# Graph-attention edge walks: the chain from logits to exponents spread over two chunks, four slots of gathered rows

## What is computed

```python
h = einsum('nd,dhf->nhf', x, W)
logits = leaky_relu(sum(h*a_src)[src] + sum(h*a_dst)[dst], 0.2)
m = segment_max(logits, dst)
e = exp(logits - m[dst])
z = segment_sum(e, dst)
out = segment_sum(h[src] * (e / (z[dst] + eps)), dst)
```

## Time and profile before

| | |
|---|---|
| median of 3 runs | 7074.7 us (7064.91 to 7080.67) |
| the profiled execution | 7060.18 us, span 7058.4 |
| PE busy | 4868.9 us (69%) |
| PE weight loads | 3367.9 (48%) |
| DVE | 3968.4 (56%) |
| ACT | 2368.3 (34%) |
| POOL | 2984.7 (42%) |
| mean granted TensorE clock | 0.815 of 2.4 GHz |
| gathers of line 783 | 832 in `l_edges`, 416 each in `l2a_edges` and `l2b_edges` |

### The profile page before, as it was taken

One profiled execution on the slowest core, in us unless ns is written; L12 is line 12 of the kernel. 1 busy time (PEld: TensorE's weight loads), 2 busy tenths in 40 slices (PEclk: granted clock), 3 DMA queues, 4 the chain that ended last, 5 costly groups with the idle time before them and its releaser, 6 DMA issues. The chain is left out here.

```text
span 7058.4 us, 80551 instructions
## 1 busy us (share of the span) xinstructions
PE 4868.9 (69%) x19231; PEld 3367.9 (48%) x19232; DVE 3968.4 (56%) x8601; ACT 2368.3 (34%) x5719; POOL 2984.7 (42%) x2932
## 2 busy tenths in 40 slices
PE   2676749547775947775577747888898555377999
PEld 2444426325543734444344434444577333265666
DVE  3555633446667246665466656667324788686333
ACT  1333312123333224433243424455221222174333
POOL 2555432445552045552655526666000777352000
PEclk8778859768787968888688868889999666697999
DMA  4454414234442034443444411111001999673000
GB/s 116 137 163 153 114 54 126 90 102 141 141 144 62 1 108 144 136 143 87 141 136 144 130 42 27 30 30 27 22 7 52 362 368 377 213 228 98 9 13 23
DMA packets 543458, 819.10 MB, mean 116 GB/s; under 512 B 87966, under 2 KB 421967, under 8 KB 542839
## 3 DMA queue, kind: packets, MB, share of 16 engines
q1 hardware_dynamic: 396388, 432.93, 19.0%
q0 software_dynamic: 140832, 376.78, 18.9%
q10 hardware_dynamic: 5907, 5.92, 0.3%
HBM read 658.06 MB, written 157.71 MB: 116 GB/s over the span
## 5 line engine op out<-in xcount | busy, mean ns | idle before, releaser
L783 POOL DMA_INDIRECT l_edges_stage<-l_h_rows,src_t x832 | 802.1, 964 | 682.7 <-issue 217.9
L1096 PE MATMUL l_edges_ps_sum<-l_edges_msg,l_edges_hot 128*128 128x264 f32 x1664 | 595.1, 500 | 275.7 <-DVE l_attn_acc L925 179.8
L2492 POOL DMA_INDIRECT l_edge_kv<-l_kv_rows,src_t x416 | 476.3, 1145 | 673.2 <-POOLq L2400 516.8
L2918 POOL DMA_INDIRECT l_gate_edges_srow<-l_gate_src_rows,l_gate_edges_idx x512 | 487.2, 952 | 329.7 <-issue 142.3
L3054 PE MATMUL l_gate_edges_ps<-l_gate_edges_wide,l_gate_edges_hot_lo 128*128 128x500 f32 x1024 | 505.6, 636 | 102.5 <-issue 72.0
L1096 PEld LDWEIGHTS l_edges_ps_sum<-l_edges_msg,l_edges_hot 128*128 128x128 f32 x1664 | 354.1, 238 | 438.0 <-DVE l_attn_acc L925 257.7
L2545 PE MATMUL l_edge_ps_q<-l_q_q,l_edge_hot 128*128 x832 | 341.2, 581 | 303.9 <-issue 211.4
L783 POOL DMA_INDIRECT l2a_edges_stage<-l2a_h_rows,src_t x416 | 400.0, 961 | 340.8 <-issue 118.1
L783 POOL DMA_INDIRECT l2b_edges_stage<-l2b_h_rows,src_t x416 | 400.7, 963 | 329.0 <-issue 116.1
L2545 PEld LDWEIGHTS l_edge_ps_q<-l_q_q,l_edge_hot 128*128 128x128 f32 x832 | 231.8, 292 | 413.2 <-issue 367.4
L1096 PE MATMUL l2a_edges_ps_sum<-l2a_edges_msg,l2a_edges_hot 128*128 128x272 f32 x832 | 303.4, 508 | 159.6 <-DVE l2a_sums_acc L925 106.9
(11 more groups left out here) (786 smaller groups left out, 10893.5 us busy)
## 6 DMA issues: line engine op xcount, KB each, us to landing
l_edge_e<-e_rows SPq DMA_DIRECT2D x416, 128.0 KB
l_val_rows<-l_edge_vj SPq DMA_DIRECT2D x104, 512.0 KB
l_agg_stage<-l_val_rows SPq DMA_DIRECT2D x52, 1024.0 KB, 5.6
l_edges_rel_b<-rel_rows SPq DMA_DIRECT2D x52, 512.0 KB
l_edges_ea<-in_edge_attr SPq DMA_DIRECT2D x48, 512.0 KB
e_rows<-l_edges_e_s SPq DMA_DIRECT2D x48, 512.0 KB
l_experts_w<-in_L_ffn_w SPq DMA_DIRECT2D x32, 512.0 KB, 5.0
l_gate_edges_lo_b<-l_gate_edges_lo_rows SPq DMA_DIRECT2D x64, 256.0 KB
```

The costliest lines, as they stand in the source:

```text
L783: nc.gpsimd.indirect_dma_start(out=stage[:, c % SL, u, :], out_offset=None, in_=h_rows, in_offset=bass.IndirectOffsetOnAxis(ap=K.src_t[:, ...
L1096: nc.tensor.matmul(ps_sum[u][:], hot[:, g, u, :], msg[:, g % 2, u, :], start=True, stop=True).then_inc(summed, 1)
L2492: nc.gpsimd.indirect_dma_start(out=kv[:, m, u, :], out_offset=None, in_=kv_rows, in_offset=bass.IndirectOffsetOnAxis(ap=K.src_t[:, n * EB ...
L2918: nc.gpsimd.indirect_dma_start(out=srow[:, n % 4, u, :], out_offset=None, in_=src_rows, in_offset=bass.IndirectOffsetOnAxis(ap=idx[:, n * ...
```

## The change

- The chain is stretched. In chunk c DVE runs `tile_tops(c+1)` right behind `rescale`, then `logits(c+2)`, weigh 1, `nodes_hot(c+3)`, the adds of group 0, weigh 2, `tile_ends(c+2)` mixed with the adds of group 1, `edge_maxima(c+1)`, weigh 3, the adds of group 2, `exponents(c+1)`, the adds of group 3. PE's products follow that order, and `expand(c+3)` stands behind the second `scatter`.
- `lgT` has two halves in `ps_w`, so that two chunks can be under way. The one semaphore that counted DVE's steps becomes four.
- `stage` has four slots (SL = 4). POOL's extra waits stay, now: group 1 of chunk c for the turned logits of c-2, group 2 for the placed tops of c-3, group 3 for the placed ends of c-2.
- `rel_b` has one slot, `e_s` half the rows (each half of a chunk's terms is stored by itself), and the zeros are a quarter as wide and sent with a repeated source.
- DVE's loop has four chunks (PER = 4) and five turns; the last six chunks are written out. PE's loop has one turn fewer.
- The first two chunks' chains run ahead of the loop.

The core of the diff (waits and scans of the same form are cut):

```diff
-    SL, PER = 3, 6
-    assert (NCK - 2) % PER == 0 and PER % SL == 0 and PER % 2 == 0
+    SL, PER = 4, 4
+    REST = 2
+    assert (NCK - REST) % PER == 0 and PER % SL == 0 and PER % 2 == 0
     with Phase(nc, name) as ph:
         stage = ph.sb("stage", [P, SL, CK, RW])
-        rel_b = ph.sb("rel_b", [P, 2, CK * P], BF16)
+        rel_b = ph.sb("rel_b", [P, CK * P], BF16)
...
-        e_s = ph.sb("e_s", [P, 2, EdgeTerms.PER_CHUNK, D])
+        e_s = ph.sb("e_s", [P, 2, EdgeTerms.PER_CHUNK // 2, D])
...
@@ -774,11 +778,11 @@
                         if c >= SL:
                             pool.wait_ge(msg_built, NG4 * (c - SL) + g + 1)
                             if g == 1:
-                                pool.wait_ge(lg_turned, c - SL + 2)
+                                pool.wait_ge(lg_turned, c - SL + 3)
                             elif g == 2:
-                                pool.wait_ge(ends_placed, c - SL + 2)
+                                pool.wait_ge(inits_made, c - SL + 2)
                             elif g == 3:
-                                pool.wait_ge(inits_made, c - SL + 2)
+                                pool.wait_ge(ends_placed, c - SL + 3)
...
-                def store(c):
-                    sp.wait_ge(e_kept, 2 * c + 3)
+                def store(c, h):
...
+                def rel(c):
+                    if c >= 1:
+                        sp.wait_ge(hotT_built, c)
+                    sp.dma_start(rel_b[:], over_partitions(K.rel_rows[c * CK:(c + 1) * CK, :].rearrange("s e -> (s e)"))).then_inc(rel_in, 16)
...
                 for c in range(NCK):
-                    if c >= 2:
-                        sp.wait_ge(hotT_built, c - 1)
...
+                    if c + 2 < NCK:
+                        rel(c + 2)
...
+                        store(-1, 1)
+                    if c >= 2:
+                        store(c - 2, 0)
+                        store(c - 2, 1)
...
                 def tile_ends(c, i, add):
                     cut_f, cut_r = (K.cuts[:, bass.ds(c, 1), a, :].rearrange("p c e -> p (c e)") for a in range(2))
                     dve.wait_ge(lg_turned, c + 1)
-                    nc.vector.tensor_tensor_scan(local[:, 1, :], cut_f, lgT, NEG, ALU.add, ALU.max).then_inc(dv, 1)
+                    if not (isinstance(c, int) and c == 0):
+                        dve.wait_ge(inits_made, c)
+                    nc.vector.tensor_tensor_scan(local[:, 1, :], cut_f, lgT[i % 2], NEG, ALU.add, ALU.max).then_inc(end_steps, 1)
...
-                def tile_tops(c, i, add):
+                def tile_tops(c, i):
...
+                def exponents(c, i, with_ends):
                     m = i % 2
+                    dve.wait_ge(f_placed, c + 1)
+                    if with_ends:
+                        dve.wait_ge(ends_placed, c + 2)
                     dve.wait_ge(max_turned, c + 1)
...
                     blks = block_ids(nc, mybir.EngineType.DVE, K, c)
                     rescale(c, blks[0])
                     if after >= 1:
-                        logits(c + 1, j, i + 1)
-                    for g, step in enumerate((tile_ends, tile_tops, edge_maxima)):
-                        weigh(c, i, g + 1)
-                        if after >= 1:
-                            step(c + 1, i + 1, adds(c, g, blks))
-                        else:
-                            for u in range(GR):
-                                adds(c, g, blks)(u)
+                        tile_tops(c + 1, i + 1)
+                    if after >= 2:
+                        logits(c + 2, j, i + 2)
+                    weigh(c, i, 1)
+                    if after >= 3:
+                        nodes_hot(c + 3, j, i + 3)
+                    for u in range(GR):
+                        adds(c, 0, blks)(u)
+                    weigh(c, i, 2)
+                    if after >= 2:
+                        tile_ends(c + 2, i + 2, adds(c, 1, blks))
+                    else:
+                        for u in range(GR):
+                            adds(c, 1, blks)(u)
                     if after >= 1:
-                        exponents(c + 1, i + 1)
-                    if after >= 2:
-                        nodes_hot(c + 2, j, i + 2)
+                        edge_maxima(c + 1, i + 1)
+                    weigh(c, i, 3)
                     for u in range(GR):
-                        adds(c, GR - 1, blks)(u)
+                        adds(c, 2, blks)(u)
+                    if after >= 1:
+                        exponents(c + 1, i + 1, after >= 2)
+                    for u in range(GR):
+                        adds(c, 3, blks)(u)
...
                 nodes_hot(0, 0, 0)
                 logits(0, 0, 0)
-                for step in (tile_ends, tile_tops, edge_maxima):
-                    step(0, 0, lambda u: None)
                 nodes_hot(1, 0, 1)
-                exponents(0, 0)
-                with dve.Fori(0, (NCK - 2) // PER) as j:
+                tile_ends(0, 0, lambda u: None)
+                tile_tops(0, 0)
+                logits(1, 0, 1)
+                nodes_hot(2, 0, 2)
+                tile_ends(1, 1, lambda u: None)
+                edge_maxima(0, 0)
+                exponents(0, 0, True)
+                with dve.Fori(0, (NCK - REST) // PER - 1) as j:
                     for i in range(PER):
-                        chunk(j * PER + i, j, i, 2)
-                chunk(NCK - 2, (NCK - 2) // PER, 0, 1)
-                chunk(NCK - 1, (NCK - 2) // PER, 1, 0)
+                        chunk(j * PER + i, j, i, 3)
+                LAST = (NCK - REST) // PER - 1
+                for i in range(PER + REST):
+                    c = LAST * PER + i
+                    chunk(c, LAST, i, min(3, NCK - 1 - c))
 
...
                 def chunk(c, m, after, j=None):
                     last_maxima(c, m, 0)
+                    if after:
+                        rescaling(c + 1, 1 - m)
                     for g in range(1, NG4):
                         if j is not None and g == 3:
                             keep_turned(c, 0)
                         edges_hot(c, g)
                         last_maxima(c, m, g)
                     if j is not None:
-                        keep_terms(c, m, 0, j * 16 + 16)
+                        keep_terms(c, m, 0, j * 32 + (16 * m + 16))
                     if after:
-                        rescaling(c + 1, 1 - m)
                         edges_hot(c + 1, 0)
                         if j is not None:
                             keep_turned(c, 1)
                         weights(c + 1)
                     if j is not None:
-                        keep_terms(c, m, 1, None)
+                        keep_terms(c, m, 1, j * 32 + (16 * m + 16))
...
                 def chunk(c, m, after, j=None):
                     scatter(c, 0)
+                    if after >= 2:
+                        turn_logits(c + 2, m)
                     if after >= 1:
-                        turn_logits(c + 1, 1 - m)
+                        place_tops(c + 1)
                     if after >= 2:
                         turn_attr(c, m, 0, j * 16 + 16 * (m + 1))
                     scatter(c, 1)
-                    if after >= 1:
-                        place_ends(c + 1)
+                    if after >= 3:
+                        expand(c + 3, m, block_ids(nc, mybir.EngineType.PE, K, c + 3))
                     if after >= 2:
                         attr_terms(c, 0)
                     scatter(c, 2)
-                    if after >= 1:
-                        place_tops(c + 1)
                     if after >= 2:
                         turn_attr(c, m, 1, None)
-                    scatter(c, 3, 0, GR // 2)
                     if after >= 1:
+                        turn_maxima(c + 1)
                         place_f(c + 1)
-                        turn_maxima(c + 1)
-                    scatter(c, 3, GR // 2)
                     if after >= 2:
-                        blks = block_ids(nc, mybir.EngineType.PE, K, c + 2)
+                        place_ends(c + 2)
+                    scatter(c, 3)
                     if after >= 2:
                         attr_terms(c, 1)
-                        expand(c + 2, m, blks)
...
                 last.then_inc(e_made, 1)
                 expand(0, 0, block_ids(nc, mybir.EngineType.PE, K, 0))
                 turn_logits(0, 0)
+                expand(1, 1, block_ids(nc, mybir.EngineType.PE, K, 1))
                 place_ends(0)
+                turn_logits(1, 1)
                 place_tops(0)
+                expand(2, 0, block_ids(nc, mybir.EngineType.PE, K, 2))
+                turn_maxima(0)
                 place_f(0)
-                turn_maxima(0)
-                expand(1, 1, block_ids(nc, mybir.EngineType.PE, K, 1))
-                with pe.Fori(0, NCK // 2 - 1) as j:
+                place_ends(1)
+                with pe.Fori(0, NCK // 2 - 2) as j:
                     for m in range(2):
-                        chunk(j * 2 + m, m, 2, j)
```

(5 more changed lines are left out.)

107 lines of the change are left out of this document (47 added, 60 removed).

## The result

The changed kernel takes 7223.67 us (median; 7216.02 to 7241.96) where the kernel before takes 7069.81: ratio 1.022, 95% interval 1.0195 to 1.0245, +154 us. The profiled execution took 7241.96 us with a span of 7240.2, against 7060.18 and 7058.4: +181.8. It was the slowest of its four, so the trace shows somewhat more loss than the medians do.

What follows compares the result with a forecast made beforehand. No engine is full in mid walk; held PE signals make chunks with gathers some 9 us longer. Middle 0, starts and ends +36, turns +17: +53 on the 7074.7 median gives 7128, forecast 7080 to 7170 (wider range 6920 to 7255).

Steps and rivals of the forecast that it cites:

- The sign and the mechanism: Whole kernel slower, +53 us; the wait at L866 moves to another DVE instruction, likely the adds of group 1.
- the hold: PE signals from about 5 us into a row of unbroken gathers are seen at 1.40 us x gathers from its start.
- The middle: Chunks in mid walk: zero change, taken between two breaks a chunk (-1.9 us) and longer runs (+1.5 to +3.5).
- the run of twelve: Rival: POOL's unbroken rows grow from eight to twelve gathers, some +1.3 us a chunk, 7232 us in all; chance 0.19.
- W2: Third of a chunk's four `weigh`: ends 8.4 us into POOL's gathers, before the eighth is issued at 9.8.
- The start: Start of each walk: four slots let 68 gathers go unbroken rather than 52; +18 us a walk, bounds +5 and +28.
- The end: End of each walk: gathers end a chunk earlier, one more chunk at 17.8 rather than 26.6 us; -9 a walk.
- Turns: DVE's loop, four chunks instead of six: one turn more a walk, +4.2 us x 4 = +17.
- DVE's order: DVE's waits on itself: some 2 us a chunk, hidden by holds, a cost below some 21 us a chunk.
- Second read port: `hotT` and gathers meeting: up to 0.53 us of POOL each, happens today too; nothing added, +10 us allowed.
- smaller buffers: `rel_b`, `e_s` and zero rows: nothing for each; if SP's order is late, the load shows before L836.

Runs made afterwards that it cites:

- a_again: The changed kernel itself, unaltered, measured again in another group where signals are held: 7221.35 us, ratio 1.0206 to the kernel before.
- a_gate_sums: Changed kernel, with POOL's group g also waiting for sums up to group g-1 of chunk c-4 (held): 7014.04 us, 0.9949 of the kernel before.
- a_all: Changed kernel with later POOL gates on sums, `expand` at chunk end, the opening gathers cut into eights, PER = 8 (held): 7053.61 us, 0.9979 of before.
- a_ng_expend: Changed kernel without the gathers of chunks 4 to 25 (output wrong), `expand` moved to the chunk's end on PE (free): 6159.01 us.
- b_gate4: Kernel before, with POOL's group g also waiting for the sums of the same group of chunk c-3 (free): 6244.42 us, 0.9992 of before.
- a_gate4_again: Changed kernel with the strict gate, group g waiting for the same group's sums of chunk c-4; repeated (free): 6394.76 us, 1.0232 of before.

## Why the prediction was right or wrong

- *The sign and the mechanism* were right: the hold left L866 and stood before the first add of group 1, ended by the end of the run, at 1.40 us a gather.
- *The middle* is the step that failed. "I take zero, the middle between this and the run of twelve": it is +28.9 us in 20 chunks of `l2a` (+23.9 in `a_again`), or some +25 and +20 without the added turn, 1.0 to 1.2 a chunk. The prediction had worked out that W2 ends 8.4 us into the run, before the eighth gather at 9.8, so that group 2 is let go at once; by its own durations the rival of the run of twelve was the likelier, and its price (+1.3 a chunk) was nearly right. Splitting the difference between two cases was the error. `a_gate_sums`, where POOL's waits alone are later, shows it: 2.5% go.
- *The rival's time*, 7232 against 7223.67, is so near in part by luck: runs are of sixteen too, PE's order was in no sum, and start and end were put too low.
- *The start*: +18 us forecast, +26.6 measured at the third rescale. The first rescale came 92.2 us behind the first gather, near the 95.5 forecast for the hold. The second came 117.3 behind it, before 95.0: 22.3 us later, so nothing of the hold was used, where 4 us had been counted on.
- *The end*: -9 forecast, -6.5 measured for the last three intervals. Over the four walks start and end cost 58.8 us (88.4 less 29.6) where the sum had 36.
- *Turns*: 3.6 us before `weigh` 0, four times a walk, near the 4.0 of the forecast's row. Twelve turns fewer in `a_all` gave 27 us, 2.3 each, about half of the 4.2.
- *DVE's order* "becomes a cost below some 21 us a chunk": without gathers a chunk does stay at 22.0 us, but the engine named was the wrong one. It is PE's order, which the prediction looked at nowhere: `expand` and `attr_terms` ahead of the third scatter (`a_ng_expend`: 19.3 us a chunk). Free, 13 us of a walk's 43.9 come with the depth of the chain, and PE's order is the likely cause of the 19.2 in the span; moving `expand` was not tried there with gathers.
- *Second read port, smaller buffers*: POOL's busy time rose by 19.2 us in all (2984.7 to 3003.9). That is less than the 78 us that would come if each meeting with `hotT` cost POOL a whole `hotT`, an estimate from the exclusive lock of which the Trainium skill speaks (SBUF — State Buffer, section "SBUF: two separate sides"). The gathers that overlap a `hotT` are together 15.2 us longer than 0.95 each in before (127 gathers) and 28.7 in after (142), so as a rule a meeting doesn't cost POOL a whole `hotT`, and the 1.48 us of the prediction's row is an extreme. No wait of weight was found behind SP's order.
- *What stays open*: what switches the hold and what makes it; how much of the held loss is PE's order (moving `expand` gives 95 us alone and takes back 0.67% with the gate, so it has no price of its own); what reading the block table earlier would give; and whether another kind of DMA would hold signals. None of these was tried.

## What to carry to other kernels

When a wait is removed, look at the next instruction on that engine that reads the same producer; and when a wait of one queue (here POOL's gates) is tied to an event that the change makes earlier, work out how long that queue then runs without a break. A reordering that spreads a chain may need the gates moved with it: held, the same chain is 2.2% slower, or with later gates, a cut start and a longer loop 1.6% faster. That isn't general: free, it is 2.3% slower with the strict gate as well. So look on every engine at what an instruction that was moved now stands ahead of, here `expand` ahead of the third scatter. Work out by your own durations which of two cases holds; don't take the middle.

## What the runs showed of the hardware

- The hold is not always there: the kernel before takes 7068 or 6248 us on one chip, and in the second condition a run of 416 gathers (`b_gate4`) holds nothing. A gather's own time is 0.95 us (median) in both.
- Where it is there, PE's own work is slowed as well: the last products of `expand` follow at 1.40 us, one a gather (from 2768.56 to 2769.96 and 2771.36).
- The same sixteen products take 0.61 us (median of 26 chunks, before), 2.1 (after's order, free: `a_gate4_again`) or up to 8.8 (after, held).
- The profile names the releaser of a held signal "remote" or some long past DMA. "Remote" alone is a sign of the condition: 599.5 us of DVE's waits in before, 854.8 in after, none in the eight free traces. It is no measure of the whole hold, for the 5 us waits at L866 stand under a DMA's name.
- The granted clock differs with the order of the same products: free, it is 0.95 in the middle in the old order (`b_gate4`) and 0.86 in the new (`a_gate4_again`); 0.96 and 0.89 without gathers.
